# Slot attention in a fused decoder: row sums in 32-row strips for two groups at once, and a last turn written out

## What is computed

```python
for _ in range(NUM_ITERS):                       # 3
    sn = rmsnorm(slots, slot_norm_w)
    q_proj = sn @ Wq.T
    scores = jnp.einsum('bkd,bmd->bkm', q_proj, k_proj) * SCALE
    attn = jax.nn.softmax(scores, axis=-2)       # over the 1024 slots
    attn = attn / (jnp.sum(attn, axis=-1, keepdims=True) + EPS)   # over the 154 rows
    updates = jnp.einsum('bkm,bmd->bkd', attn, v_proj)
    slots = gru_cell(updates, slots, gru_wih, gru_whh, gru_bih, gru_bhh)
```

## Time and profile before

| | us |
|---|---|
| median of 3 runs | 1556.6 (1555.96 to 1561.25) |
| the profiled execution, whole time | 1547.12 |
| its span | 1545.4 |
| slot stage, first to last of the three turns on PE | 48.9 to 389.2 |
| one turn, from first score block to first score block | 113.1 |
| PE busy, share of the span | 84% |
| DVE busy, share of the span | 50% |

### The profile page before, as it was taken

One profiled execution on the slowest core, in us unless ns is written; L12 is line 12 of the kernel. 1 busy time (PEld: TensorE's weight loads), 2 busy tenths in 40 slices (PEclk: granted clock), 3 DMA queues, 4 the chain that ended last, 5 costly groups with the idle time before them and its releaser, 6 DMA issues.

```text
span 1545.4 us, 18867 instructions
## 1 busy us (share of the span) xinstructions
PE 1297.7 (84%) x6050; PEld 760.5 (49%) x6051; DVE 771.4 (50%) x2122; ACT 437.5 (28%) x842; POOL 290.6 (19%) x310
## 2 busy tenths in 40 slices
PE   5999999999348799899998639999768889799993
PEld 3534334334234344444443526667545555688862
DVE  7373573563964255556652502222266563255546
ACT  2212212212052244435434103333132211233320
POOL 2100100100121000000000031111011555155550
PEclk9999999999677699999998569999875689899997
DMA  9999992000100000000100851110106622355536
GB/s 314 338 337 330 330 334 87 0 0 0 30 25 1 1 1 1 0 1 1 31 1 1 309 196 34 34 34 29 64 31 208 204 83 89 98 160 158 157 120 263
DMA packets 136659, 171.35 MB, mean 111 GB/s; under 512 B 8464, under 2 KB 124944, under 8 KB 136464
## 3 DMA queue, kind: packets, MB, share of 16 engines
q1 hardware_dynamic: 126992, 143.81, 30.2%
q0 software_dynamic: 9600, 26.65, 4.8%
HBM read 68.11 MB, written 102.32 MB: 110 GB/s over the span
## 4 chain that ended last, share of the span: by engine, by line
PE 69%; DVE 16%; ACT 4%; DMA 3%; issue 3%; POOL 3%; SPq 2%; DVEq 0%; ACTq 0%; POOLq 0%
PE psum L1873 11%; PE psum L1212 5%; PE psum L1196 5%; PE psum L2046 5%; PE psum L1000 5%; PE psum L2102 3%; PE psum L1864 2%; PE psum L1017 2%; DVE arena L2626 2%; DVE arena L2448 2%; PE psum L2079 2%; PE psum L2032 2%; PE psum L2126 2%; PE psum L1901 2%; POOL xs L870 2%
## 5 line engine op out<-in xcount | busy, mean ns | idle before, releaser
L1873 PE MATMUL psum<-arena 128*128 128x512 f32 x432 | 206.4, 617 | 0.0
L2626 DVE TENSOR_REDUCE arena<-psum 128x4 f32<-128x616 f32 x128 | 102.1, 798 | 126.9 <-PE psum L2046 125.6
L2046 PE MATMUL psum<-arena 32*128 32x308 f32 x512 | 112.0, 516 | 24.2 <-DVE arena L2626 22.9
L1873 PEld LDWEIGHTS psum<-arena 128*128 128x128 f32 x432 | 79.0, 195 | 97.8 <-issue 97.8
L1140 POOL DMA_INDIRECT ys<-xnT,arena x96 | 92.1, 960 | 104.6 <-DVE xnT L1106 82.1
L2220 ACT ACTIVATE arena<-psum,arena 128x512 f32<-128x512 f32 x72 | 49.1, 686 | 192.0 <-PE psum L1873 180.1
L2334 ACT ACTIVATE arena<-psum 128x2048 f32<-128x2048 f32 x40 | 75.0, 1874 | 76.9 <-PE psum L2083 59.9
L1000 PE MATMUL psum<-arena,xn 128*128 x384 | 90.7, 390 | 1.4 <-ACT xn L1051 0.9
L1212 PE MATMUL psum<-arena,xn 128*128 x384 | 88.6, 385 | 2.0 <-ACT xn L1258 2.0
L1196 PE MATMUL psum<-arena,side 128*128 x192 | 88.1, 602 | 1.0 <-ACT side L1251 0.6
L2046 PEld LDWEIGHTS psum<-arena 32*128 32x128 f32 x512 | 41.9, 200 | 92.1 <-DVE arena L2626 61.4
(11 more groups left out here) (397 smaller groups left out, 2245.8 us busy)
## 6 DMA issues: line engine op xcount, KB each, us to landing
xs<-zeros SPq DMA_DIRECT2D x8, 8576.0 KB, 59.5
arena<-in_W SPq DMA_DIRECT2D x16, 1024.0 KB, 14.0
xn<-xs SPq DMA_DIRECT2D x96, 134.0 KB, 2.3
arena<-in_gate_up SPq DMA_DIRECT2D x4, 2048.0 KB, 15.7
arena<-ys SPq DMA_DIRECT2D x4, 2048.0 KB, 15.3
arena<-in_down SPq DMA_DIRECT2D x4, 1024.0 KB, 15.4
xs<-zeros SPq DMA_DIRECT2D x1, 3120.0 KB, 16.4
side<-xs SPq DMA_DIRECT2D x24, 130.0 KB, 2.2
```

The costliest lines, as they stand in the source:

```text
L1873: ins = pe.matmul(bank[dict(hn=4, r=5, z=6, xn=7)[k]][:], lhs[:, cols], r, start=(start and n == 0), stop=(stop and n == len(w) - 1))
L2046: ins = pe.matmul(bank[4 + i][:, 0:2 * M].rearrange("p (h m) -> p h m", h=2), qhT[rows, n % 3, c, t * P:(t + 1) * P], keys[rows, l, c, b, ...
L2626: dve.tensor_reduce(neg[:, n % 2, t, 2 * pair:2 * pair + 2, 2 * c:2 * c + 2], psum[:, 4:6, 0:2 * M].rearrange("p b (h m) -> p b h m", h=2) ...
```

## The change

Its parts:

1. **Row sums in strips.** `row_sums(b)` now does both groups of a batch. Each group's sum is a matmul with 32 columns of weights, so group q's sums stand on 32 partitions of bank 1, at 32q. The rest uses the copy of `e_rem` at 32 times the group's number in the batch. DVE adds 1e-6 (`row_sums_kept`) and takes the reciprocal (`row_sums_inverted`) for two groups in one 64x512 instruction each. `spread_sums(b)` then spreads each group's 32 equal rows over 128 partitions with a matmul against `share32` (1/32 everywhere), into banks 0, 2, 3 and 1, from which `attention(q)` multiplies directly. `sinv_rep` is 32 columns wide.
2. **Spreading with two banks.** `spread_group` alternates between banks 1 and 0.
3. **Start of a turn.** The score block of group q waits for its own slots only, and for the reading of the banks that it overwrites. For that the `gate_read` semaphores start at 8.
4. **Square sums together.** They come in one piece between `recurrent_part(q, 1)` and `input_part(q, 1)`.
5. **Last turn.** The loops run two turns; the third is written out behind them, without squares and square sums for a next one.

```diff
-                    if q == 0:
-                        pe.wait_ge(h_ready, it * 8 + 2)
-                    elif q == 1:
-                        pe.wait_ge(h_ready, it * 8 + 8)
+                    pe.wait_ge(h_ready, it * 8 + 2 * q + 2)
+                    if q == 1:
+                        pe.wait_ge(gate_read["hn"], it * 8 + 8)
+                        pe.wait_ge(gate_read["r"], it * 8 + 8)
                     elif q == 2:
                         for _ in square_sums(it, G - 1):
                             pass
+                        pe.wait_ge(gate_read["z"], it * 8 + 8)
+                        pe.wait_ge(gate_read["xn"], it * 8 + 8)
...
-                    if j >= 1:
-                        pe.wait_ge(spread_copied, it * 8 + j)
-                    pe.matmul(bank[1][:], ones[:], diag[:, q % 2], start=True, stop=True).then_inc(spread_ready, 1)
+                    if q >= 2:
+                        pe.wait_ge(spread_copied, it * 6 + q - 1)
+                    pe.matmul(bank[(q + 1) % 2][:], ones[:], diag[:, q % 2], start=True, stop=True).then_inc(spread_ready, 1)
...
+                def row_sums(b):
+                    pe.wait_ge(sinv_spread, it * B + b + 1)
+                    if b == 0:
+                        pe.wait_ge(spread_copied, it * 6 + 4)
+                    for i in range(GB):
+                        q = b * GB + i
+                        pe.matmul(bank[1][32 * q:32 * q + 32], sinv_rep[:, 0, b], e_main[:, b, i * GN:(i + 1) * GN],
+                                  start=True, stop=False, tile_position=(0, 32 * q))
+                    for i in range(GB):
+                        q, rows = b * GB + i, slice(32 * i, 32 * i + MR)
+                        ins = pe.matmul(bank[1][32 * q:32 * q + 32], sinv_rep[rows, 1, b], e_rem[rows, b, i * GN:(i + 1) * GN],
+                                        start=False, stop=True, tile_position=(32 * i, 32 * q))
+                    ins.then_inc(spread_ready, 1)
+                def spread_sums(b):
+                    pe.wait_ge(spread_copied, it * 6 + 4 + b + 1)
+                    for q in range(b * GB, (b + 1) * GB):
+                        rows = slice(32 * q, 32 * q + 32)
+                        ins = pe.matmul(bank[sums_bank[q]][:], share32[rows], inv_row[rows], start=True, stop=True,
+                                        tile_position=(32 * q, 0))
+                    ins.then_inc(spread_ready, 1)
...
-                    recurrent_part(q, 1, sums)
-                    input_part(q, 1, sums)
+                    recurrent_part(q, 1)
+                    if it is not last_turn:
+                        for _ in square_sums(it + 1, q - 1):
+                            pass
+                    input_part(q, 1)
+
+            with pe.Fori(0, ITERS - 1) as it:
+                turn(it)
+            turn(last_turn)
```

More of the change, by code:

```diff
@@ L174, in build @@
         cand = carve(2 * GN).rearrange("p (q n) -> p q n", q=2)
+        inv_row = spread[:, 0]
+        share32 = carve(P)
         small = carve(256)
@@ L1711, in slot_iterations_gpsimd, with turn @@
                 squares(0, q, first=(q < 2))
-            with pool.Fori(0, ITERS) as it:
+            def turn(it):
                 squares(it, G - 1)
@@ L1720, in slot_iterations_gpsimd @@
                                        ALU.mult).then_inc(vws_ready, 1)
-                for q in range(G - 1):
-                    squares(it + 1, q)
+                if it is not last_turn:
+                    for q in range(G - 1):
+                        squares(it + 1, q)
+            with pool.Fori(0, ITERS - 1) as it:
+                turn(it)
+            turn(last_turn)
         def mha_rows_gpsimd(pool, l):
@@ L1921, in slot_iterations_tensor @@
                 row_sums(0)
+                recurrent_part(0, 0, blocks=("z",))
                 row_sums(1)
-                row_sums(2)
                 recurrent_part(0, 1, blocks=("hn",))
+                spread_sums(0)
                 input_part(0, 0)
                 recurrent_part(0, 1, blocks=("r", "z"))
-                row_sums(3)
                 input_part(0, 1)
+                spread_sums(1)
                 for q in range(1, G):
@@ L2199, in slot_iterations_scalar, with turn @@
         def slot_iterations_scalar(act):
-            act.wait_ge(c_rms, 3)
-            with act.Fori(0, ITERS) as it:
+            act.wait_ge(c_rms, 4)
+            def turn(it):
                 def copy_spread(q):
                     act.wait_ge(spread_ready, it * 8 + q + 1)
-                    act.activation(spread[:, q], bank[1][:], ACT.Copy).then_inc(spread_copied, 1)
+                    act.activation(spread[:, q], bank[(q + 1) % 2][:], ACT.Copy).then_inc(spread_copied, 1)
                 def exponentials(b):
@@ L2240, in slot_iterations_scalar @@
                     candidate(q, 1)
+            with act.Fori(0, ITERS - 1) as it:
+                turn(it)
+            turn(last_turn)
         def ternary_scalar(act):
@@ L2371, in context_slots_vector @@
         def context_slots_vector(dve):
+            dve.memset(share32, 1.0 / 32).then_inc(c_rms, 1)
             dve.memset(kqR[:], 0.0).then_inc(c_rms, 1)
@@ L2497, in slot_iterations_vector @@
                 ch.close()
+            with dve.Fori(0, ITERS - 1) as it:
+                turn(it)
+            turn(last_turn)
         def unpack_ternary_vector(dve):
```

96 lines of the change are left out of this document (49 added, 47 removed).

## The result

| | before | after |
|---|---|---|
| median of 14 runs each | 1559.88 us | 1549.95 us |
| ratio, with its 95% interval | | 0.9933 (0.9906 to 0.996) |
| start of DVE's L2505, after: L2555, `unpacked`, the first work behind the slots | 394.17 us | 386.66 us |

The change makes the kernel faster by some 10 us, not by 27. The time lies outside the predicted range of 1522 to 1542 us.

What follows compares the result with a forecast made beforehand. PE's time line was taken as the bound, with DVE counting only where PE waits. The terms 2.9 + 7.3 + 11.0 + 0.5 + 5.4 = 27.1 us came off the 1556.6 us median, giving 1529.5 us, range 1522 to 1542 us.

Steps and rivals of the forecast that it cites:

- Start of a turn: Turns 1 and 2: PE's wait before group 1's scores goes, POOL is late next; gain 1.47 us a turn, 2.9 us.
- Spreading: Third to fourth score block in three turns: 9.88 us shrinks to 7.45, gaining 2.43 us a turn, 7.3 us.
- The middle: Fourth score block to input_part(1, 0): 38.9 us becomes 35.65; 3.25 us in turns 1 and 2, 4.5 in turn 0, 11.0 together.
- the two bounds: DVE's reciprocal of 64 partitions in the middle: between 1.7 us and the full 3.35 us; the full one was taken.
- Square sums together: Square sums in one piece take 1.70 us instead of costing 1.8 us a group; gain 0.5 us over two turns.
- Last turn: The last turn's square sums go: 3 x 1.8 = 5.4 us of PE, on the path.
- a stall at the step into the written-out turn: Rival at the last turn's start: stalls for its code, some 4 us, giving 1533.5 us; chance 0.05.
- the clock falls all the same: Rival in the middle's two waits: one fall of 1.5 to 1.7 us a turn, 5 us, 1534.6 us; chance 0.12.
- slower: Rival: clock drops at the 0.95 us wait, stays down over thin 32-column work; up to 63 us more, 1593 us; chance 0.03.
- strips to one bank take turns: Rival in the row sums: rest matmuls writing one bank go serially, 1.7 us a turn, 5.1 us, 1534.6 us; chance 0.13.

Runs made afterwards that it cites:

- E8: The kernel before with only the spreading alternating between two banks; 1542.43 us against 1546.27 us for before, ratio 0.9978.
- E3: The changed kernel with an unused matmul of ones in both middle waits, ahead of row_sums(0) and input_part(0, 0); 1544.5 us against before's 1560.95 us, 0.9879.
- E1: The changed kernel run again, unchanged; 1546.43 us against 1560.95 us for before, ratio 0.9900.
- E11: The kernel before with the row sums in strips, keeping the changed gate_read counts and last turn written out for DVE and ACT; 1555.55 us against before's 1558.99 us, 1.0001.
- E7: The kernel before with only the square sums in one piece, in all three turns; 1550.13 us against 1546.27 us for before, ratio 1.0038.
- E6: The kernel before with the last turn written out for PE and POOL only; 1541.93 us against 1546.27 us for before, ratio 0.9970.
- E2: The changed kernel with the square sums of turns 0 and 1 back between the matmuls; 1544.67 us against 1560.95 us for before, ratio 0.9897.
- E5: The changed kernel with square sums between the matmuls again and both middle waits filled; 1529.43 us against 1546.27 us for before, ratio 0.9896.
- E9: E5 with the steps of square sums starting only at block r; 1535.29 us against 1558.99 us for before, ratio 0.9876.
- E10: The changed kernel with only the second wait filled, one matmul before input_part(0, 0); 1541.61 us against 1558.99 us for before, ratio 0.9893.
- E4: The changed kernel with groups 0 to 2's square sums for the next turn cut to one matmul each (wrong norms); 1532.85 us against before's 1560.95 us, 0.9810.

## Why the prediction was wrong in size

Point by point, in its own steps:

1. **Start of a turn (2.9 us): half right.** The wait is gone, POOL is late next, and the square sums start 7.18 us behind group 0's block (163.13 to 170.31); 7.19 was worked out. But the third score block then ran at the low clock in both turns, 1.7 us each, and takes the gain back. Before had a wait of 1.53 us in the score blocks *ahead* of the piece, and the clock stayed up; after has 0.16 us of wait, and it fell. That is the opposite of what idle time alone would do. No run undid this part alone.
2. **Spreading (7.3 us): right.** 59.19 to 66.46 is 7.27 us, where 7.45 was worked out. In turns 1 and 2 it is 8.97 us (172.26 to 181.23), the same 7.27 and the 1.7 us of the fall of point 1. The fourth block itself takes 3.71 us, not the 3.43 booked. E8, which has it alone, shows the same distance, and that a third of the gain is lost later in the turns.
3. **The middle (11.0 us): the mechanism right, the size not.** Without falls it is 36.0 us long (E3) against 35.65 worked out. The reciprocal of 64 partitions took 3.35 us, the upper of the two bounds. The write of 32 columns (L2475, 1.50 us) does end with POOL's. The waits were as long as forecast. What failed is the sentence that such waits are too short to matter, which rested on one counterexample, the 1.53 us wait of the earlier trace rows. Of the 11 us, 5.8 were the removal of before's falls (1.5 us in turns 1 and 2, 2.75 in turn 0), and falls came back at the same place: 3.3 to 5.1 us a turn in after's first profile, 1.65 in E1, and up to 1.7 in E11. Before's own are 1.7 us, and 2.9 in turn 0.
4. **Square sums together (0.5 us): wrong in sign.** E7 alone is slower by 1.0038 (1.0021 to 1.0055). The step was priced by how long the thin matmuls take, 1.70 against 4 x 0.45 us, and not by what comes behind them.
5. **Last turn (5.4 us): right.** 379.07 is followed by six instructions in 2.79 us, no L1842 stands in it, and E6 has 5.4 us for it in its chain and 4.3 us in the medians. The rival of a stall at the step into the written-out turn fell with it.

**The step that failed** is the clock, which the sum puts at nothing: point 3 takes full clock behind its two waits, on the strength of one row, and points 1 and 4 book nothing at all for what runs behind a piece of square sums. The runs showed falls at up to four places in a turn, of 1.65 to 3.4 us each, 18.5 us in one execution and 15.1 in another of the 27.1 booked. The prediction named a part of it as the rival *the clock falls all the same*, with a chance of 0.12, and priced that at one fall of 1.5 to 1.7 us a turn, 5 us; it looked for falls at the waits only. The *slower* rival, in which the low clock lasts over 40% of the thin work, didn't happen: the four L1885 behind the second row sums are back at 1.92 us at 82.51.

The rival *strips to one bank take turns* fell. The chain has 0.98 us for four L1931 instructions that write one bank from two row strips and two column strips; one after the other would be 1.7 us. By the Trainium skill's page TensorEngine Tiling (Array Packing), section Restrictions and Gotchas, different row tiles can't use one PSUM bank at the same time. This trace doesn't agree where the column strips differ as well.

**What is shown and what isn't.** Shown in the chains: taking the pieces apart removes the falls at the turn ends (E2, E5, E9), filling the second wait removes that behind it (E3, E5, E9, E10), and with both the end of the slots moves by 9 to 15.5 us against the changed kernel. Also shown: the pieces alone cost time in the old kernel (E7). That filling the first wait does anything is not shown: without a filling 2 of 18 such waits were followed by a fall, with it none of 9.

Each chain is one execution, but the counts over all profiles agree. The second wait of the strips is followed by a fall in 11 of 15 cases unfilled and in none of 12 filled. The last piece of 16 in a turn is followed by one in all 11 cases (after, E1, E3, E7, E10), the same thin matmuls spread out never. The whole times carry less: the ratios of E2, E3, E5, E9 and E10 can't be told from E1's 0.9900, and only E4's lies lower. Their medians do go with the slots. The time from turn 0's third score block to the end of the slots and the median are below before's by 10.9 and 14.5 us in E1, 17.7 and 16.5 in E3, 17.6 and 17.4 in E10, 19.8 and 16.8 in E5, 23.8 and 23.7 in E9, and 33.7 and 28.1 in E4.

The Trainium skill's page TensorE: Matmul & The Clock Gate, Part 1, has the clock follow how busy PE has lately been. The traces agree at the second wait, which is followed by a fall when PE idles 1.38 us in it and by none when it is filled. For the square sums they differ from what the profile's own busy share would suggest: it books the 16 instructions as busy throughout (1.68 us), and the clock fell behind them.

Open: why one piece or wait is followed by a fall and the next one not. Of the three pieces in a turn the last always had one, the second never (136.43 and 249.28 in after), and the first in 3 of 11 cases (both in E1, one in E3). The piece at a turn's start had one in 13 of 16 cases with the new start of a turn (170.31 and 283.12 in after) and in none of 12 with the old one. The three without are the two of E4, where the pieces before them were gone, and that of turn 2 in E9 (272.62), whose order there is the same as at the start of turn 1, which had one. No run varied the distance between a piece and the thin or idle stretches before it by itself, and so this wasn't tried.

## What to carry to other kernels

Price every edit on TensorE at both clock levels: ask not only how long the thin matmuls or the wait take, but what wide work stands right behind, since that is what pays. Scatter thin matmuls between wide ones, and try a wide matmul without use in a wait that is followed by a fall; in this kernel the one in the wait of 1.38 us gave 5.0 us by the end of the slots (E3 against E1), more than many a shortening. Read such a result at the end of the changed stage: the unchanged rest of a single execution moved by 18 us between the two profiles here, nearly twice what the change was worth.

## What the runs showed of the hardware

- DVE's SCALAR_TENSOR_TENSOR with two operands in SBUF, 128x512, took 2.34 us when it started beside POOL's 1.89 us L1710 (E5, above, and at 110.67 and 223.52 in after); before's mean for it is 0.689 us and after's 0.828, with the two slow ones among 24:

```profile
L2500 DVE SCALAR_TENSOR_TENSOR arena<-arena 128x512 f32<-128x512 f32 x24 | 19.9, 828 | 94.1 <-ACT arena L2251 94.1
```

- A wide matmul added in the second wait shortens what follows (14 instructions in 6.21 us, E3 and E10, in place of 7.65, E1); thin ones packed together at a turn's end lengthen it (six in 4.48 us, E7, in place of 2.79).
- DVE's reciprocal of 512 numbers on 64 partitions took 3.35 us, as long as on 128.
- The seven unchanged sub-layers took between 1149.7 us (E7) and 1172.6 us (E3) in single executions, 1151.2 and 1157.7 us in before's own two. What sets this was not tried.
